# Logits matmuls spread over steps 2 to 4, row turns set before the third tile of the maximum pass, second group ranked in batch 14

## The reference, cut to what matters

```python
x = x + tanh(g_xattn[0]) * xattn(layernorm(x), ctx, ctx)     # 64 small heads of depth 4 and 8
x = x + tanh(g_ffn[0]) * ffn(layernorm(x), wg, W, b)
# ffn
xt = x.reshape(-1, 512)
logits = xt @ wg                                   # (2048, 8)
probs = softmax(logits); idx = argmax(probs); gate = probs[idx]
out = gate * (xt @ W[idx].T + b[idx])
```

## Time and profile before

| what | us |
|---|---|
| median of 3 runs | 586.19 |
| lowest and highest | 584.19, 586.42 |
| profiled execution, its own time | 586.99 |
| span of the profiled execution, first to last instruction | 585.4 |

### The profile page before, as it was taken

The page is one execution under the profiler, slowest core; times in us unless marked ns, Lnnn a source line. Parts: engine busy times, 40 slices in busy tenths (PEclk is TensorE's granted clock), DMA queues, the critical chain, the costliest instruction groups (busy, mean ns, idle before and its releaser), DMA issues.

```text
span 585.4 us, 9717 instructions
## 1 busy us (share of the span) xinstructions
PE 524.5 (90%) x2603; PEld 178.2 (30%) x2603; DVE 442.1 (76%) x868; ACT 349.5 (60%) x429; POOL 369.9 (63%) x630
## 2 busy tenths in 40 slices
PE   0489999899999999999989999999998989899993
PEld 0012223232323232322323232323232235345451
DVE  5897898888898988989898989898998575112121
ACT  3227686868687777778676868776666842111110
POOL 7455577857675866767666787786555446544531
PEclk9999999999999999999999999999999989999997
DMA  4865547775757476554627354535331054633410
GB/s 141 236 151 184 171 151 205 231 201 163 198 160 234 133 210 179 190 181 128 198 63 215 113 167 108 165 98 139 93 108 40 25 181 165 194 129 101 137 40 0
DMA packets 39077, 86.74 MB, mean 148 GB/s; under 512 B 12498, under 2 KB 14546, under 8 KB 39008
## 3 DMA queue, kind: packets, MB, share of 16 engines
q1 hardware_dynamic: 26944, 61.17, 36.4%
q0 software_dynamic: 12096, 25.13, 13.5%
HBM read 63.24 MB, written 28.18 MB: 156 GB/s over the span
## 4 chain that ended last, share of the span: by engine, by line
PE 45%; DVE 36%; issue 7%; POOL 4%; ACT 4%; DMA 3%; POOLq 0%; DVEq 0%; ACTq 0%; SPq 0%
DVE neg_max L862 23%; PE ps_pv L1243 13%; PE ps_ring L1202 11%; PE ps_scores L1302 10%; PE ps_scores L1224 6%; ACT probs L779 3%; DVE neg_max L1075 3%; PE ps_pv L1252 2%; DVE den_turned L888 1%; PE ps_scores L1283 1%; DMA stacks<-shift_parts 1%; PE ps_pv L1260 1%; DVE st L904 1%; PE ps_ring L1210 1%; DVE st L873 1%
## 5 line engine op out<-in xcount | busy, mean ns | idle before, releaser
L862 DVE TENSOR_REDUCE neg_max<-ps_ring 128x1 f32<-128x512 f32 x480 | 312.3, 681 | 42.5 <-PE ps_ring L1202 41.7
L779 ACT ACTIVATE probs<-ps_scores 128x1024 f32<-128x1024 f32 x256 | 250.0, 1021 | 72.0 <-PE ps_scores L1224 69.4
L1202 PE MATMUL ps_ring<-stacks 96*128 96x512 bf16 x480 | 180.2, 388 | 16.0 <-DVE neg_max L862 5.8
L1224 PE MATMUL ps_scores<-stacks 128*128 128x512 bf16 x512 | 153.9, 383 | 4.7 <-ACT probs L779 2.8
L1243 PE MATMUL ps_pv<-probs,v_ones 128*32 128x512 f32 x1024 | 137.9, 611 | 0.3 <-DVE logits L914 0.3
L1202 PEld LDWEIGHTS ps_ring<-stacks 96*128 96x128 bf16 x480 | 46.1, 96 | 191.5 <-DVE neg_max L862 173.1
L1302 PE MATMUL ps_scores<-w_sb,f_xt 128*128 x184 | 83.2, 593 | 0.0
L1224 PEld LDWEIGHTS ps_scores<-stacks 128*128 128x128 bf16 x512 | 48.1, 101 | 49.6 <-ACT probs L779 16.1
L556 POOL DMA_DIRECT2D stacks<-shift_parts x96 | 49.4, 518 | 20.6 <-POOL shift_parts L547 17.6
L772 ACT COPY f_xt<-ps_scores 128x512 f32<-128x512 f32 x23 | 13.5, 586 | 71.9 <-PE ps_scores L1283 71.9
L1302 PEld LDWEIGHTS ps_scores<-w_sb,f_xt 128*128 128x128 f32 x184 | 34.4, 190 | 33.0 <-issue 32.2
(11 more groups left out here) (144 smaller groups left out, 509.2 us busy)
## 6 DMA issues: line engine op xcount, KB each, us to landing
stacks<-parts_dram SPq DMA_DIRECT2D x224, 64.0 KB, 2.6
parts_dram<-prep POOLq DMA_DIRECT2D x15, 768.0 KB
w_sb<-w_t SPq DMA_DIRECT2D x16, 512.0 KB, 6.1
recs_dram<-rec SPq DMA_DIRECT2D x16, 512.0 KB, 4.3
stacks<-parts_dram SPq DMA_DIRECT2D x32, 192.0 KB, 3.1
prep<-x_perm SPq DMA_DIRECT2D x16, 256.0 KB, 3.1
prep<-k_perm SPq DMA_DIRECT2D x16, 256.0 KB, 3.4
v_in<-v_t SPq DMA_DIRECT2D x16, 256.0 KB, 3.5
```

Source lines behind the costliest of these rows:

```text
L779: nc.scalar.activation(probs[:, k % 2, 2 * jp:2 * jp + 2], ps_scores[:, jp], ACT.Exp).then_inc(exp_done, 1)
L862: nc.vector.tensor_reduce(neg_max[:, g, j, c:c + 1], ps_ring[:, u.slot(n)], AX.X, ALU.max, negate=True).then_inc(ring_free, 1)
L1202: nc.tensor.matmul(ps_ring[:, u.slot(n + c)], q_stack[0:KS, B.p, g, j, c * 128:(c + 1) * 128], k_stack[0:KS, B.p, g, j], start=True, stop= ...
L1224: last = nc.tensor.matmul(ps_scores[:, jp, j % 2], k_stack[0:KA, B.p, g, j, c * 128:(c + 1) * 128], q_stack[0:KA, B.p, g, j], start=True, ...
```

## The change

- The four matmuls of `route(B-2)` leave the end of step 0. They stand between tiles 1 and 2 of the maximum pass: chunk 0 in step 2, chunk 1 in step 3, chunks 2 and 3 in step 4. In batches 10 and 14, which rank a group, all four stand in step 2.
- They write bank 1 of `ps_pv` (`routed_bank`) rather than bank 0. So the first of them waits for `high_read` of batch B-1, and the values of step 5 (the first into bank 1) wait until DVE has taken the logits.
- DVE takes the logits at (4, 3), or at (2, 3) in batches 10 and 14.
- `turn_rows(B-1)` moves from behind the values of step 7 to between tiles 1 and 2 of step 7.
- `find_experts` moves from (1, 1) to (5, 0), the exponentials of the gates on ACT from step 2 to step 6, `find_gates` from (5, 0) to (4, 1).
- Group 1 is ranked in batch 14 instead of 13. `take_ranks`, `find_gates` and `count_tiles` all stand in step 4 of batch 14 then, and POOL numbers the group and issues its four stores there in one piece, behind `copy_values` of batch 15. Before, it issued two in batch 13 and two in batch 14.

```diff
-RANKED = (10, 13, 15, None)
+RANKED = (10, 14, 15, None)
...
-        rows_bank, ranks_bank = ps_pv[:, 0], ps_pv[:, 1]
+        rows_bank, routed_bank, ranks_bank = ps_pv[:, 0], ps_pv[:, 1], ps_pv[:, 1]
...
# POOL
-                if B.known(ROUTED[1] + 1):
-                    store_tokens(GROUPS[1][0] + 2, GROUPS[1][1])
                 split_maxima(B.plus(1), 0)
...
-                if B.known(ROUTED[1]):
+                if B.known(RANKED[1]):
                     number_places(1)
-                    store_tokens(GROUPS[1][0], GROUPS[1][0] + 2)
+                    store_tokens(*GROUPS[1])
                 spread_sums(B, 0)
-                if B.known(ROUTED[1] + 1):
+                if B.known(RANKED[1]):
                     read_slots(0)
...
# ACT
-                        if k == 2 and B.known(ROUTED[group]):
+                        if k == 6 and B.known(ROUTED[group]):
                             exp_gates(group)
...
# DVE
                         if prev2:
-                            if at == (1, 0):
-                                take_logits(B.plus(-2))
+                            ranked = B.known(RANKED[0]) or B.known(RANKED[1])
+                            if at == ((2, 3) if ranked else (4, 3)):
+                                take_logits(B.plus(-2), routed_bank)
...
-                            if B.known(ROUTED[group]) and at == (1, 1):
+                            if B.known(ROUTED[group]) and at == (5, 0):
                                 find_experts(group)
                             if B.known(RANKED[group]) and at == (4, 0):
                                 take_ranks(group, ranks_bank)
-                            if B.known(RANKED[group]) and at == (5, 0):
+                            if B.known(RANKED[group]) and at == (4, 1):
                                 find_gates(group)
-                        if B.known(ROUTED[1] + 1):
+                        if B.known(RANKED[1]):
                             if at == (4, 2):
                                 count_tiles(0)
...
# PE, values: g is the half of the steps
                     if g == 0 and (not isinstance(B.b, int) or B.b > 1):
+                        pe.wait_ge(rows_taken, B.b - 1)
+                        if B.known(NB - 1):
+                            pe.wait_ge(logits_taken, B.b - 1)
+                    if g == 1 and (not isinstance(B.b, int) or 1 < B.b < NB - 1):
                         pe.wait_ge(logits_taken, B.b - 1)
...
+            def route(B, bank, chunks=range(NC)):
+
+                if 0 in chunks:
+                    pe.wait_ge(rows_taken, B.b + 1)
+                for c in chunks:
+                    last = nc.tensor.matmul(bank[:, 0:NE], xt[:, c], wg_sb[:, c], start=c == 0, stop=c == NC - 1)
+                if NC - 1 in chunks:
+                    last.then_inc(logits_full, 1)
+
+            def fill(B, k):
+
+                ranked = B.known(RANKED[0]) or B.known(RANKED[1])
+                if k == 2:
+                    pe.wait_ge(high_read, B.b)
+                    route(B.plus(-2), routed_bank, range(NC) if ranked else (0,))
+                if k == 3 and not ranked:
+                    route(B.plus(-2), routed_bank, (1,))
+                if k == 4 and not ranked:
+                    route(B.plus(-2), routed_bank, (2, 3))
...
                     if nxt:
-                        scores_for_max(B.plus(1), u, n - 1, k, (1, 2))
-                        n += 2
+                        scores_for_max(B.plus(1), u, n - 1, k, (1,))
+                        n += 1
+                        if prev2:
+                            fill(B, k)
+                        if k == 7 and prev:
+                            turn_rows(B.plus(-1))
+                        scores_for_max(B.plus(1), u, n - 2, k, (2,))
+                        n += 1
...
-                    if k == 7 and prev:
+                    if k == 7 and not nxt:
                         turn_rows(B.plus(-1))
...
-                    if k == 0 and prev2 and nxt:
-                        route(B.plus(-2))
```

More of the change, by code:

```diff
@@ L736, in take_rows @@
                 act.wait_ge(rows_full, B.b + 1)
+                wait(act, logits_full, B.b)
                 nc.scalar.copy(xt[:].rearrange("p c n -> p (c n)"), rows_bank).then_inc(rows_taken, 1)
@@ L909, in mean2, with take_logits @@
                 nc.vector.bn_aggr(mv2[:], st2[:]).then_inc(ln2_stats, 1)
-            def take_logits(B):
+            def take_logits(B, bank):
                 dve.wait_ge(logits_full, B.b + 1)
                 nc.vector.tensor_copy(logits[:, bass.ds(B.b, 1)].rearrange("p o e -> p (o e)"),
-                                      rows_bank[:, 0:NE]).then_inc(logits_taken, 1)
+                                      bank[:, 0:NE]).then_inc(logits_taken, 1)
             def wide(ap, n, e):
@@ L1101, in end @@
                 take_columns(0)
-                take_logits(B.plus(-2))
+                take_logits(B.plus(-2), rows_bank)
                 find_experts(2)
@@ L1173, in _ @@
             invert_sums(last, 1)
-            take_logits(last.plus(-1))
+            take_logits(last.plus(-1), rows_bank)
             turn_back(last)
@@ L1179, in _ @@
                 if s == 2:
-                    take_logits(last)
+                    take_logits(last, rows_bank)
                     find_experts(3)
@@ L1254, in turn_rows @@
                 last.then_inc(rows_full, 1)
-            def route(B):
-                pe.wait_ge(rows_taken, B.b + 1)
-                for c in range(NC):
-                    last = nc.tensor.matmul(rows_bank[:, 0:NE], xt[:, c], wg_sb[:, c], start=c == 0, stop=c == NC - 1)
-                last.then_inc(logits_full, 1)
+            def route(B, bank, chunks=range(NC)):
[14 more added lines that the diff above has]
+                    route(B.plus(-2), routed_bank, (2, 3))
             def rank(group, bank):
@@ L1338, in emit @@
                     if k == 1 and not nxt:
-                        route(B.plus(-2))
+                        route(B.plus(-2), rows_bank)
                     if nxt:
-                        scores_for_max(B.plus(1), u, n - 1, k, (1, 2))
-                        n += 2
+                        scores_for_max(B.plus(1), u, n - 1, k, (1,))
[6 more added lines that the diff above has]
+                        n += 1
                     if k > 0:
@@ L1348, in emit @@
                         if k == 3 and B.known(RANKED[group]):
-                            pe.wait_ge(high_read, B.b)
+                            pe.wait_ge(logits_taken, B.b - 1)
                             rank(group, ranks_bank)
@@ L1370, in _ @@
             turn_slot(1, ps_xt[:, 1])
-            route(last.plus(-1))
+            route(last.plus(-1), rows_bank)
             def turn_next(s):
@@ L1380, in _ @@
                 if s == 2:
-                    route(last)
+                    route(last, rows_bank)
                 if s == 1:
```

## The result

| | before | after |
|---|---|---|
| median, us (4 runs each, in turns) | 585.57 | 590.76 |
| lowest and highest, us | 584.19, 586.42 | 590.17, 592.23 |
| profiled execution, its own time and its span, us | 586.99, 585.4 | 590.39, 588.8 |

The ratio after to before is 1.009, interval 1.007 to 1.011. The forecast was 588.0 from 586.19, a change of +1.8 us, with a range of 583.9 to 590.9. The measured change is +5.2. That the time itself, 590.76, still lies inside the range by 0.1 is luck: the kernel before measured 0.6 lower in these runs, and neither of the rivals for which the upper end was drawn, the unusable holes and the late table, came true.

The account below looks back on a forecast made before the run. Attention batches alternate between DVE and PE, neither alone the bound, so their waits count. Terms 1.1 - 0.29 (batch 1) - 0.9 + 0.9 - 0.27 + 1.27 gave +1.8 us on the median 586.19: 588.0, range 583.9 to 590.9.

Parts of the forecast that it names:

- the unusable holes: Rival, steps 2 and 3: next tile's weights load only behind the logits, up to 0.20 each, 592.4 us; chance 0.08.
- the late table: Rival, batch 14: POOL's four stores delay the slot table's read, +2 to +5 us, 590 to 593; chance 0.11.
- the term of batch 9: Moved `find_experts`, 0.6 exposed where 1.62 was before: -0.9 us, up to +0.1 if POOL's next subtraction has begun.
- Plain batches: Batches 2 to 8, 11, 12: step 4 logits cost 0.41, turned rows gain 0.29; +0.12 each, +1.1 us together.
- The rows: Step 7: turned rows of 0.50 us fill 0.29 of idle PE and push 0.21; gain 0.29 a batch.
- Steps 2 and 3, step 0: Logits cost 0 in the holes of steps 2 and 3; leaving step 0 gains 0, except 0.25 in batches 13, 14.
- step 0 was PE's: Rival: PE had been the bound in step 0, so 0.81 falls out of thirteen batches, 577.5 us; chance 0.03.
- Small matmuls nearly free: Rival, step 4: the logits' cost of 0.41 falls out of eleven batches, 583.5 us; chance 0.11.
- The copy of the logits: DVE's copy before step 5's tile 2: taken as 0; rival 0.15, with step 4 dearer by 0.2, 590.5 us, chance 0.12.
- Batch 10: Logits in step 2 0.52, copy 0.05, `find_gates` in step 4 0.62, turned rows -0.29: +0.9 us.
- Batch 13: `find_experts` at 0.41 and the batch's other terms sum to 0.28, against 0.55 before: -0.27 us.
- Batch 14: Step 2 logits 0.52, copy 0.05, rows -0.29, step 0 -0.25, rank matmuls 0.14, DVE's step 4 work 1.1: +1.27 us.

Follow-up runs that it names:

- e1_hold: The changed kernel; in batch 9 POOL starts its two `lows` subtractions only after DVE's one-hot of group 0. Ratio to the kernel before 1.0018, median 587.01 us.
- e2_warm: The changed kernel; the four value matmuls of step 4 of batch 9 are made four times over, with the same result. Ratio 1.0046, median 588.19 us.
- e4_back: The changed kernel with the turned rows back behind the values of step 7. Ratio 1.0157, median 594.68 us.
- e3_turn: The kernel before with one edit: the turned rows between tiles 1 and 2 of step 7. Ratio 0.9933, median 581.34 us.
- e6_two_hold: The changed kernel with POOL's wait for the one-hot in batch 9, logits chunks in pairs in steps 2 and 3, none in step 4. Ratio 0.9965, median 583.84 us.
- e7_gates: The changed kernel with POOL's wait for the one-hot in batch 9 and `find_gates` back at (5, 0). One execution: batch 10 27.63 us for 28.21.
- e5_turn_hold: The kernel before with turned rows between tiles 1 and 2 of step 7, and POOL's `add_attention` in batch 9 waiting for the one-hot. Ratio 0.9922, median 581.28 us.
- e10_reduce: The changed kernel with the one-hot of group 0 made by one TENSOR_REDUCE, without a POOL wait. One execution: batch 9 27.43 us.
- e8_scalar: The changed kernel with the one-hot of group 0 made by eight instructions, each one SBUF tensor and one value per partition. One execution: batch 9 33.03 us.
- e9_one_input: The changed kernel with the one-hot of group 0 made by eight instructions comparing one SBUF tensor with a constant. One execution: batch 9 32.61 us.
- e11_between: The changed kernel; in batch 9 POOL's second subtraction, not the first, waits for the one-hot of group 0. One execution: batch 9 30.20 us.

## Why the prediction was wrong

**The step that failed** is the term of batch 9: "At (5, 0) POOL issues transfers, so I take 1.2 for eight batches of logits", with -0.9 for the batch and "Bounds: the same 1.62 again, which makes it +0.1". The runs showed +3.87. The hold was named there, but two things were wrong in its price.

- *What runs beside it.* I looked at what POOL does at the start of `find_experts`, and bounded the hold by the one instruction of the earlier trace rows. `find_experts` takes about 1.2 us, its last instruction is the one that matters, and POOL's two subtractions of `lows` stand right behind the transfers. The bound should have been all that POOL runs in one piece there, 2.27 us, and the lead of 0.42 before it: the instruction took 2.78. Without the hold the term was nearly right: 28.57 to 27.43 in e1_hold is -1.14, against -0.9.
- *What the stall does to PE.* I priced a stall at its own length, since the clock was at 1.00 throughout. In the pause of 2.94 the granted clock fell to its lower level, and e2_warm puts that at 2.4 us, nearly as much again; e4_back, with the same pause, at 1.3.

**The rest of the sum, term by term.**

- *Plain batches:* right mechanism, sizes off. Step 4 0.37 for 0.41, turned rows -0.35 for -0.29. Nine batches give +0.3, not +1.1. At 26.99 the plain batch lies within the 26.9 to 27.2 that the prediction named: its own sign of being wrong did not show.
- *The rows* gain more than the hole of 0.29: e3_turn has 0.36. They push tile 2 by 0.15, not by 0.21.
- *Steps 2 and 3, step 0:* 0 and 0, as forecast. The rival that the holes can't be used is refuted, also for a pair (e6_two_hold, 0.06 each). The rival that step 0 was PE's is refuted by e3_turn.
- *Small matmuls nearly free:* refuted by e4_back, 0.37 for four records.
- *The copy of the logits:* nothing. L913 runs at 195.17, with the next maximum right behind. (The rival that priced it, with step 4 dearer by 0.2, does not add up as written: nine batches at 0.35 are 3.2, not 2.5.)
- *Batch 10:* +0.74 for +0.9. Step 2 grew by 0.53 for the forecast 0.52, and `find_gates` cost 0.58 by e7_gates for the forecast 0.62.
- *Batch 13:* -0.15 for -0.27. `find_experts` of group 1 cost 0.46 in step 1 and costs 0.69 in step 5.
- *Batch 14:* +0.89 for +1.27. Step 0 gives -0.22 for -0.25, step 2 +0.53 for 0.57, step 7 -0.35 for -0.29. Step 4 was too large: it grew from 4.57 to 5.34, 0.77 for the 1.1 of `take_ranks` and `find_gates`.
- *Late slot table:* refuted, L1032 without idle.

The forecast sum without batch 9 was 1.8 + 0.9 = 2.7 us; measured it is 5.3 - 3.87 = 1.4. Had batch 9 given the forecast -0.9, the batches would have made +0.5 us; e1_hold, which has the hold taken out, came to a ratio of 1.0018. So the terms other than batch 9 were together 1.3 us too high, and that hid a part of the miss of 4.8 in batch 9. The prediction knew the hold, as a bound of batch 9; none of its rivals had one of 2.78 us, or a fall of the clock.

**What the change is worth.** Turned rows between tiles 1 and 2 gain 0.36 in each batch. The logits lose 0.37 because half of them stand in step 4, which has no hole, and gave nothing back where they stood before. In batches 10 and 14 all of them in step 2 lose 0.53. The moves of `find_experts` and `find_gates` lose the rest. The fastest versions leave out all but the rows: e3_turn and e5_turn_hold, 0.7% and 0.8% under the kernel before.

## What to carry to other kernels

Before moving a small instruction on DVE, look at what POOL runs from its start until its *last* instruction is through, and take all that POOL does without a pause as a careful bound of a hold; its kind may be changed (e10_reduce) as well as its place. A stall that stops PE can have a second price, the clock behind it (1.3 to 2.4 us here), and the rows of an undisturbed kernel don't show it. Work moved into a hole must come from a place where it was paid for: 0.8 us of logits beside DVE work were free, and half of them in a step without a hole cost 0.37.

## What the runs showed of the hardware that I had not expected

- A DVE instruction of some 0.2 us lasted 2.73 to 2.81 us although its record starts 0.42 or 0.43 *before* that of POOL's subtraction, in the kernel after, e2_warm, e4_back, e8_scalar and e9_one_input; 1.69 in e11_between, where POOL paused. The Trainium skill (SBUF — State Buffer, "SBUF: two separate sides") gives the ports to whichever starts first, for one instruction. By these records the second to start had them, and where its two subtractions followed without a pause it kept them over both. That POOL takes them earlier than its record begins would fit; no run tests it.
- It is not always so. In the kernel before, the one-hot of group 1 (403.84) starts 0.12 ahead of a subtraction of POOL (403.96), for which POOL had waited 0.93 on ACT, and takes 0.19: not held. In the kernel after, the same one-hot (419.22) lasts 0.38 beside two copies of POOL that follow without a pause (419.14 and 419.48), and ends 0.05 behind the first, not behind the second. What makes the difference is open.
- The granted clock does not go by the length of PE's pause alone. It stayed at 1.00 behind 1.43 (before, batch 9), 1.24 (after, batch 14) and 2.13 us (e5_turn_hold, at 461.9). It was at 0.50 for some 3.4 us at or behind 1.23 (e1_hold, batch 14), 1.85 (e11_between) and 2.95 (e4_back), and for 6.7 us at 2.94 (after) and 3.40 (e9_one_input). In the kernel after it fell within the pause, in e11_between just after it; either way most of the loss lies in steps that have nothing to do with the stall.
- Four small matmul records cost 0.37 where PE is what is waited for, and 0.06 in a hole of 0.29 that they overfill.
